# A Flamingo block on one core: the attention's softmax shifts are transposed in fp32 and split behind the transposition

## The reference

```python
def attn(query, key, value, mask, Wq, bq, Wk, bk, Wv, bv, Wo, bo):   # 16 heads of 8 channels
    q, k, v = proj(query, Wq, bq), proj(key, Wk, bk), proj(value, Wv, bv)
    scores = einsum('bhqd,bhkd->bhqk', q, k) / sqrt(8)
    scores = where(mask == 0, -1e10, scores)
    return (softmax(scores) @ v) @ Wo + bo
x = x + tanh(g_xattn) * attn(layernorm(x), ctx, ctx, mask, ...)
x = x + tanh(g_ffn) * ffn(layernorm(x), ...)   # 2 shared experts (mean) + top 2 of 8 experts, gelu, 128-512-128
```

## Time and profile before

| | |
|---|---|
| three runs, us | 524.61 median (524.55 to 527.96) |
| profiled execution, span, us | 524.9 |
| PE busy | 415.9 us, 79% |
| VectorE busy | 397.8 us, 76% |
| ScalarE busy | 340.8 us, 65% |
| GpSimd busy | 315.9 us, 60% |

### The profile page before, as it was taken

How to read it: one execution, slowest core, us unless ns; L and a number is a source line. 1 busy time by engine, 2 the same in 40 slices (tenths; PEclk the granted TensorE clock), 3 DMA queues, 4 the chain that set the end, 5 groups by cost and what they waited for, 6 DMA issues and landing times.

```text
span 524.9 us, 13531 instructions
## 1 busy us (share of the span) xinstructions
PE 415.9 (79%) x4611; PEld 297.2 (57%) x4611; DVE 397.8 (76%) x983; ACT 340.8 (65%) x674; POOL 315.9 (60%) x382
## 2 busy tenths in 40 slices
PE   0377979879998989776784989898999989998930
PEld 0245767758776877554341433344878777776720
DVE  7696769868778778987774896494888768886795
ACT  0536857657787877665663876495677567765743
POOL 9151524494987889598876376650466656666550
PEclk9998989899999999988997989999999999999985
DMA  8767863442333534540011011113122222244119
GB/s 226 223 197 202 223 146 80 103 101 75 78 87 84 114 82 142 178 164 17 26 51 45 27 41 41 47 36 81 36 78 77 70 72 86 67 132 138 58 44 280
DMA packets 71753, 53.19 MB, mean 101 GB/s; under 512 B 7473, under 2 KB 63548, under 8 KB 71688
## 3 DMA queue, kind: packets, MB, share of 16 engines
q1 hardware_dynamic: 64608, 42.96, 30.2%
q0 software_dynamic: 4544, 8.44, 4.6%
q10 hardware_dynamic: 2536, 0.94, 0.7%
HBM read 29.38 MB, written 24.33 MB: 102 GB/s over the span
## 4 chain that ended last, share of the span: by engine, by line
PE 25%; DVE 8%; issue 5%; another core or an unknown queue 5%; ACT 4%; POOL 2%; DMA 1%; ACTq 0%; DVEq 0%; POOLq 0%
PE pAtt L1123 9%; PE pE L1111 4%; PE pS L1111 4%; DVE HH L1490 3%; PE pAtt L1061 2%; PE pMix L1101 2%; PE pS L999 2%; ACT H L767 1%; POOL yd L622 1%; PE pE L999 1%; DVE HH L1486 1%; ACT G L803 1%; DMA YY<-yd 1%; DVE t_X L1543 1%
## 5 line engine op out<-in xcount | busy, mean ns | idle before, releaser
L622 POOL DMA_INDIRECT yd<-Y,XR x78 | 85.0, 1089 | 72.5 <-DVE Y L1529 45.4
L1234 DVE TENSOR_REDUCE t_MX<-pS 128x4 f32<-128x512 f32 x128 | 86.4, 682 | 24.0 <-PE pS L861 22.4
L720 ACT ACTIVATE PT<-pE,t_mbias,t_scl 128x512 f32<-128x512 f32 x128 | 97.1, 788 | 6.6 <-PE pE L861 6.4
L597 POOL DMA_INDIRECT xs<-t_STG,t_pos x64 | 64.2, 1002 | 36.5 <-issue 15.4
L1123 PE MATMUL pAtt<-t_W2h,HR 128*128 x624 | 65.3, 219 | 6.8 <-issue 5.5
L803 ACT ACTIVATE G<-pS,t_b1T,t_inv 128x256 f32<-128x256 f32 x78 | 40.0, 569 | 43.6 <-remote 39.3
L1490 DVE SCALAR_TENSOR_TENSOR HH<-H,t_sc,HH 128x512 f16<-128x512 f32 x64 | 48.4, 761 | 21.6 <-ACT HH L772 14.7
L1521 DVE SCALAR_TENSOR_TENSOR HR<-G,t_sc,HR 128x512 f16<-128x512 f32 x78 | 58.6, 751 | 2.8
L1123 PE MATMUL pAtt<-t_W2l,HR 128*128 x312 | 56.4, 219 | 3.4 <-issue 3.4
L1123 PEld LDWEIGHTS pAtt<-t_W2h,HR 128*128 128x128 f16 x624 | 50.0, 97 | 12.6 <-issue 10.9
L861 PE MATMUL pE<-t_Q,t_K 128*128 128x128 f16 x512 | 51.6, 225 | 5.8 <-DMA t_Q<-MPT 4.8
(11 more groups left out here) (276 smaller groups left out, 1044.5 us busy)
## 6 DMA issues: line engine op xcount, KB each, us to landing
xs<-t_padrow SPq DMA_DIRECT2D x10, 516.0 KB, 5.3
XR<-xs SPq DMA_DIRECT2D x39, 129.0 KB
scr<-QKS SPq DMA_DIRECT2D x16, 256.0 KB, 2.2
t_Q<-scr SPq DMA_DIRECT2D x16, 256.0 KB
t_K<-scr SPq DMA_DIRECT2D x32, 128.0 KB
t_STG<-in_W SPq DMA_DIRECT2D x7, 512.0 KB, 6.4
YY<-yd SPq DMA_DIRECT2D x14, 256.0 KB, 5.8
t_X<-in_x SPq DMA_DIRECT2D x4, 512.0 KB, 6.5
```

Source lines behind the costliest of these rows:

```text
L597: g.indirect_dma_start(k.xs, bass.IndirectOffsetOnAxis(ap=pos[:, n:n + 1], axis=0), k.PAY[:, n, :], None).then_inc(h.di[q], 16)
L622: g.indirect_dma_start(k.yd, bass.IndirectOffsetOnAxis(ap=XR[u][:, q, D:ROW], axis=0), Y[u][:, q, :], None, bounds_check=2 * T - 1, oob_is ...
L720: act.activation(PT[:, m % NPT], pE[g % 2][:], ACT.Exp, bias=k.mbias[:, bt:bt + 1], scale=k.scl[:, bt:bt + 1]).then_inc(s.exp, 1)
L1234: v.tensor_reduce(out=MX[:, n % G // 4, m % 2, m // 2::2], in_=pS[n % 2][:], axis=AX_X, op=ALU.max).then_inc(s.max, 1)
```

## The change

The fp32 maxima are transposed as they are, and the split into high and low parts happens behind the transposition, in [16 x 256] form.

- MX has two buffers, by pair. NM and MP are gone.
- PE, at the same place of its order, transposes MX (fp32, 128x16, two of them) into rows 0 to 15 of pA[1] (pAtt). It waits for the eighth maximum and for AK of an earlier pair.
- ScalarE, at the same place, writes the high rows: fp16 of -x/32768, 16x256. They lie in the first 16 partitions of `constk` or `constq`, two constants of the prologue, by the turn's parity.
- VectorE, behind the maximum of g = 4 (of g = 3 in turn 2), writes the low rows MPl from PSUM in one operation, -x/32768 less the high part (L1244). It waits for ScalarE's high rows.
- SP issues two DMAs of two rows each, the first behind ScalarE, the second behind VectorE.
- The first weighted values of a pair's second batch, which go into pA[1], also wait for the low rows. The waits for ScalarE's copy in `transposes` and `transpose_rows` go.
- The mask rows of Q hold 4096 where they held 32768; those of K stay, from the new tile `constk`, which GpSimd fills in the prologue. The clamp at -2^29 goes.

```diff
@@ -44,7 +44,7 @@
-SCORE_TOP = float(2 ** 29)
+MASK16 = BIG16 / HD
@@ -140,7 +140,8 @@
-                g.memset(k.constq[:], BIG16)
+                g.memset(k.constq[:], MASK16)
+                g.memset(k.constk[:], BIG16)
@@ -172,7 +173,7 @@
                 for u in range(NB):
-                    a.dma_start(k.K[u][SHIFT + 2:SHIFT + 4, 1::2, :], k.constq[0:2 * HD, :]).then_inc(k.s_padk, 16)
+                    a.dma_start(k.K[u][SHIFT + 2:SHIFT + 4, 1::2, :], k.constk[:]).then_inc(k.s_padk, 16)
                 a.wait_ge(s.rest, 16 * len(rest))
@@ -258,7 +259,8 @@
-    MPT = [bg(f"MPT{u}", [4 * HD, 2, S], F16) for u in range(2)]
+    in_pair = lambda t: t[0:2 * HD].rearrange("p (a b) -> p a b", a=2)
+    MPT = [[in_pair(hi), bg(f"MPl{u}", [2 * HD, 2, S], F16)[:]] for u, hi in enumerate((k.constk, k.constq))]
@@ -299,7 +301,7 @@
-    shifts16 = pM[0:4 * HD, 0, :].bitcast(F16)
+    shifts = pA[1][0:2 * HD, 0:2, :]
@@ -315,7 +317,7 @@
-    N_W, N_RD, N_M = 16 * 3, 16 * 4, 16
+    N_W, N_RD, N_M = 16 * 3, 16 * 4, 16 * 2
@@ -462,8 +464,9 @@
                     v = (t - 2) % NB
-                    sp.wait_ge(s.t2, t - 1)
-                    sp.dma_start(k.Q[v][SHIFT:SHIFT + 4, :, :], MPT[t % 2][:].rearrange("p a b -> p (a b)")).then_inc(s.m[v], 16)
+                    for n, done in ((0, s.t2), (1, s.mp)):
+                        sp.wait_ge(done, t - 1)
+                        sp.dma_start(k.Q[v][SHIFT + n:SHIFT + 4:2, :, :], MPT[t % 2][n].rearrange("p a b -> p (a b)")).then_inc(s.m[v], 16)
                 if a:
@@ -658,7 +661,7 @@
                     act.wait_ge(s.m[(t - 4) % NB], N_M * ((t - 4) // NB) + N_M)
-                act.activation(MPT[t % 2][:].rearrange("p a b -> p (a b)"), shifts16, ACT.Copy).then_inc(s.t2, 1)
+                act.activation(MPT[t % 2][0], shifts, ACT.Copy, scale=-1.0 / BIG16).then_inc(s.t2, 1)
 
@@ -829,7 +832,6 @@
                 wait(pe, s.vev, i)
-                wait(pe, s.t2, i - 2)
                 wait(pe, l.gate, before)
@@ -892,6 +894,8 @@
                     wait(pe, s.at, 2 * pair + bb - 1)
+                    if bb == 1:
+                        pe.wait_ge(s.mp, min(pair + 2, NP))
                 if g == 0:
@@ -906,11 +910,10 @@
             def transpose_shifts(t, a):
-                pe.wait_ge(s.mp, t - 1)
-                if a:
-                    pe.wait_ge(s.vev, t + 1)
+                pe.wait_ge(s.max, G * (t - 1))
+                wait(pe, s.at, 2 * (t - LAG))
                 for bb in range(2):
-                    ins = pe.transpose(shifts16[:, S * bb:S * bb + S], MP[:, bb].rearrange("p a b c -> p (a b c)"), k.ident16[:])
+                    ins = pe.transpose(shifts[:, bb, :], MX[:, t % 2, bb].rearrange("p a b -> p (a b)"), k.identf[:])
                 ins.then_inc(s.nmT, 1)
@@ -933,7 +936,6 @@
                 pe.wait_ge(s.qk32, min(p + 10, NP))
-                pe.wait_ge(s.t2, min(p + 7, NP))
                 for part in range(2):
@@ -1231,16 +1233,15 @@
-                v.tensor_reduce(out=MX[:, n % G // 4, m % 2, m // 2::2], in_=pS[n % 2][:], axis=AX_X, op=ALU.max).then_inc(s.max, 1)
-
-            def less_maxima(pair):
-
-                n = pair + 1
-                v.wait_ge(s.max, G * n)
-                link(v.tensor_scalar(NM[:], MX[:], -SCORE_TOP, -1.0 / BIG16, ALU.max, ALU.mult))
-                wait(v, s.nmT, n - 1)
-                link(v.tensor_copy(MP[:, :, :, 0, :], NM[:]))
-                v.tensor_tensor(MP[:, :, :, 1, :], NM[:], MP[:, :, :, 0, :], ALU.subtract).then_inc(s.mp, 1)
+                if n % G == 0:
+                    wait(v, s.nmT, n // G - 1)
+                v.tensor_reduce(out=MX[:, n // G % 2, n % G // 4, m % 2, m // 2::2], in_=pS[n % 2][:], axis=AX_X, op=ALU.max).then_inc(s.max, 1)
+
+            def less_maxima(t):
+
+                hi, lo = MPT[t % 2]
+                v.wait_ge(s.t2, t - 1)
+                v.scalar_tensor_tensor(out=lo, in0=shifts, scalar=-1.0 / BIG16, in1=hi, op0=ALU.mult, op1=ALU.subtract).then_inc(s.mp, 1)
@@ -1438,9 +1439,9 @@
                         second_scales()
-                    if g == PH and b:
-                        less_maxima(t - 2)
                     maximum(G * (t - 1) + g - PH)
+                    if b and g == (PH if t < LAG else PH + 1):
+                        less_maxima(t)
                     if g == 0 and t > LAG + 1:
...
```

More of the change, by code:

```diff
@@ L250, in layer @@
     UNITS = len(SPLITS)
-    MX, NM, MP, PV, REC, AK, AT, ST6, XF, mxw, tmpn, tmpv, Cb, sel, cntp, cnti, upto, tri, O1, O2, tmp, G2 = (
-        k[n] for n in "MX NM MP PV REC AK AT ST6 XF mxw tmpn tmpv Cb sel cntp cnti upto tri O1 O2 tmp G2".split())
+    MX, PV, REC, AK, AT, ST6, XF, mxw, tmpn, tmpv, Cb, sel, cntp, cnti, upto, tri, O1, O2, tmp, G2 = (
+        k[n] for n in "MX PV REC AK AT ST6 XF mxw tmpn tmpv Cb sel cntp cnti upto tri O1 O2 tmp G2".split())
     m1, m2, ix, ex = (k[n] for n in ("m1", "m2", "ix", "ex"))
@@ L1585, in program @@
         k.keep = outer
-        alloc(outer, k, MX=([P, 2, 2, HD], F32), NM=([P, 2, 2, HD], F32), MP=([P, 2, 2, 2, HD], F16), PV=([P, 2, 2, S], F32),
+        alloc(outer, k, MX=([P, 2, 2, 2, HD], F32), PV=([P, 2, 2, S], F32),
               REC=([P, 2, H], F32), AK=([P, 2, H, HD], F32), AT=([P, 2, S], F32), ST6=([P, 2, 6], F32), XF=([P, 2, D], F32),
@@ L1594, in program @@
               bvc=([P, 1], F32), bo=([P, D], F32), bo2=([P, D], F32), rWf=([P, E], F32), bqk=([P, 2], F32), bqkr=([P, 2], F32), mx=([P, 9], F32), mxa=([P, 5], F32), mxc=([5, 1], F32), mxd=([5, 5], F32),
-                  maskr=([B, S], I32), maskf=([B, S], F32), kmrow=([B, S], F16), st=([P, NT, 6], F32), constq=([P, W2T], F16),
+                  maskr=([B, S], I32), maskf=([B, S], F32), kmrow=([B, S], F16), st=([P, NT, 6], F32), constq=([P, W2T], F16), constk=([2 * HD, W2T], F16),
                   tops=([P, TOPS], F32), rows=([P, TOPS * P], F32),
```

## The result

| | before | changed |
|---|---|---|
| median of 4 runs, us | 526.29 (524.55 to 528.07) | 520.68 (519.59 to 521.69) |
| ratio, 95% interval | | 0.989 (0.985 to 0.993) |
| span of the profiled execution, us | 524.9 | 519.8 |

The forecast was 520.9, in a range from 514.5 to 527. With a fourth run the median of before has moved from 524.61 to 526.29, so the ratio is the better measure: 0.989 is 5.8 us, where I had 3.7. That the forecast 520.9 and the median 520.68 agree so closely is luck. A second comparison of the two kernels (12 runs of the changed one) gave 0.995 (0.9925 to 0.9976), 2.4 us. So the kernel is faster, by 2 to 6 us by these two medians.

The account below looks back on a forecast made before the run. The prediction took no single engine as the bound; the end hung on when VectorE's t_nmr is ready for GpSimd, near 215.9 us. Its terms summed to 3.7 us, off the 524.61 median: 520.9 us, range 514.5 to 527.

Parts of the forecast that it names:

- The end hangs on t_nmr: GpSimd's wait for VectorE's t_nmr near 215.9 us fixes the kernel's end; PE's 3.54 us stall behind it is worth nothing.
- VectorE's exchange: Per attention turn, three VectorE operations (995 ns by the means) go and one of 0.40 us comes.
- the slower kernel that I had worked out from it: By the skill's rule VectorE loses 0.11 us a turn, 1.8 us in all: 526.4 us.
- In 14 of the turns VectorE is not the last to arrive: VectorE's own saving counts only in two turns, those of 165 and 211, worth 0.9 and 0.14 us.
- rival D: VectorE sets every turn's pace and its new operation is dearer, 0.68 against 0.54 us: 526.8 us; chance 0.07.
- The terms, in stretches: How much earlier t_nmr comes, by PE stall or VectorE saving: 0.6 + 0.56 + 0.3 + 0.9 + 0.57 + 0.63 + 0.14 us.
- queue step: In SP's queue, the store of the small weight maxima goes 1.03 us later (1.75 − 0.72), taken off a 1.58 us stall.
- My own signs: Expected in the profile: no L916 wait above 0.2 us, L1244 at 0.35 to 0.5, GpSimd's L547 near 212.3, PE's L961 near 257.
- rival B: Absorbed: PE waits as long for the next maximum, ScalarE's exponentials or GpSimd instead: 524.3 us; chance 0.14.
- SP's two DMAs: Low rows go 1.75 us after the transposition's start T; about 2 us of slack; later Q and K load costs nothing.
- A: All of it comes through: the fixed points give way and PE's stalls go whole, 9.7 us: 514.9 us; chance 0.20.
- C: The low rows' DMA lands late and PE stands at the first group in 14 other turns: 531.6 us; chance 0.09.

Follow-up runs that it names:

- N: A measure, not a run: start of GpSimd's last row waiting for t_nmr, less start of PE's first transposition of the attention; first profiles 197.9 us before, 192.8 changed.
- before's second profile: Profile of the kernel before, unchanged, run again against itself among the experiments: ratio to before 1.000 (0.998 to 1.002).
- the best version: Changed kernel with the broadcast of the weight maxima behind the two shift DMAs and VectorE's second scales three steps later: ratio to before 0.986 (0.983 to 0.9885).

## Why the prediction was right

**The end hangs on t_nmr: right.** 5.1 us earlier there, 5.0 at L961, 5.1 at the end, and 3.2 us given away behind it cost nothing that can be seen.

**VectorE's exchange: right in size.** 0.40 forecast, 0.41 measured. By the Trainium skill's rule (VectorE: DVE Perf Modes, the TRN2 errata) the estimate is 392 ns for the new operation, and the trace agrees with 401 to 413. For the old three it gives 94 ns each. They take 170 ns at their shortest, and beside GpSimd's work up to 1.03 us. With 281 ns for the three in place of the 995 of the earlier trace rows, the slower kernel that I had worked out from it did not come.

**"In 14 of the turns VectorE is not the last to arrive, so the difference matters only through PE's stall": wrong in its cause.** With the stall taken away and the operations left, N is that of before, 197.4 for 191.1 without them. VectorE's queue ahead of the next maximum sets the pace at this place in every turn where the stall was seen. This is rival D's mechanism; it came out as a gain because the new operation is cheaper than the old. It also stands where VectorE soon has time to spare (in turn 9 of the change it idles 0.47 us for PE two maxima later, at 131.95), but what that place is worth by itself no run shows. The sum survived since each stall of L913 was about the size of the three operations that PE waited for.

**The terms, in stretches.** Up to the first wait for t_nmr, 124.62 before and 121.97 now, the gain is 2.7 us where I had 0.6. From there to 171.59: 1.2, where I had 0.56 + 0.3 + 0.9 = 1.8. From there to 216.00: 1.2, where I had 1.34. So the mis-sized term is the first. Its queue step was about right: the store of the maxima stood 3.80 us behind the transposition (97.65 − 93.85) and now stands 4.67 behind it, 0.87 more for the 1.03 forecast. But the transposition itself came 2.5 us earlier (93.85 and 91.32) and not 1.58. Counted from PE's first transposition, the change is 0.5 us behind before in turn 2, 0.6 behind in turn 4, 1.0 ahead in turn 5 and 2.6 ahead in turn 6. So turn 6 gave what I had for it, and 1.6 us came between turns 4 and 5, for which I had no term. At the store the lead is 1.7 us, and 1.0 more came from there to the first t_nmr: the broadcast's rows were back 4.0 us behind its issue (105.96 to 109.92), where before took 5.2 (107.73 to 112.90).

Two things that I left out may have a share in this, and neither is shown. One is turn 2, whose stall before, 1.57 us, bears ScalarE's name in the first profile and this in the second:

```profile
46.51 0.39 PE L913 MATMUL pMix<-t_ident,t_MP 128*32 128x128 f16 x2 [1.44 <-DVE t_MP L1243]
```

It is 0.78 in the change. I had read the releaser and left the stall out. Yet in turn 2 the change is 0.5 us behind in the first pair and 1.7 ahead in the second, so its worth is open. The other is the clock: the first profile of before has 0.83 from 70 to 80 and 0.66 from 95 to 100, the changed kernel 1.00 in both, and the 1.6 us between turns 4 and 5 fall there. But before's second profile has 1.00 from 70 to 80 and from 95 to 100, and N's early part is shorter by 2.8 us in that pair too. How much the clock gave is open.

**My own signs.** L1244 at 0.41 us without idle time, two waits for the low rows' DMA and no others, GpSimd's row at 210.94 for 212.3 and PE's at 255.70 for 257: these came. Three spoke against me. PE waited 0.8 us at L916 in turn 2. The waits for `t_MX` grew by 2.2 us, so a part of rival B is real. And the granted clock fell where it had been full: from 110 to 115 it is 0.59 in the change and was 1.00 before. The prediction had priced the clock at nothing and would have called that a sign of being wrong. Before's second profile has 0.63 in the same stretch, so two executions of one kernel differ as much, and the term stays unmeasured.

**SP's two DMAs: right that they do not decide, wrong that nobody waits for the loads behind them.** K's load shows 1.2 and 1.9 us of waits in the two profiles of the change and 3.7 in the best version. That the low rows go at T + 1.75 was right for most turns, and wrong for turns 12 and 16 (4.3 and 3.1), where VectorE's inverse deviations stand before them.

**The rivals.** A: refuted, turn 17's 3.5 us were worth nothing that can be seen. B: in part, 2.2 us of waits for the maxima came back, but t_nmr moved. C: not in the change; it takes one maximum more. D: its mechanism, with the other sign.

## What to carry to other kernels

When an engine waits for the last of several operations, look at what is queued behind them on the engine that does them: if the waiting engine needs that next, taking the wait away alone moves the stall by one step, and what is to be gained is the operations' own time. Price small SBUF-to-SBUF operations of VectorE by where GpSimd works, not by their mean: here 0.18 us alone and up to 1.03 beside it, and with PSUM sources they were steady at 0.18 to 0.19. A DMA with slack can be split, but what stands behind it in its queue pays, and a load that another engine needs later should not stand ahead of a short one that is needed now.

## What the runs showed that I had not expected

The experiments' runs of both kernels were 40 us shorter than the first ones, 484.6 for 526.3 us of before. The attention is not where it lies: N is 197.1 and 197.9. From L961's row to the end before took 264.2 us in the first profile and 225.7 in the second. The first pair's traces have waits that end on "remote" in the experts' stages, as this of before, and the later ones have none there:

```profile
ACT G L803 <- remote: 39.3, 12, 3.6
```

What they are no run here shows. This one is in both kernels alike (39.5 us in the change); another differs (ScalarE's H, 17.0 us before and 7.2 after). But from L961's row on the first pair's two kernels took the same time, 264.2 and 264.1 us, so the difference between them does not come from there. In times from mixed comparisons a 1% gain would be unreadable.
